# Attention scores in 64-row halves, product weights in 32-column tiles, and the values of two key tiles in one go

## The chip, the cores and the metric

The kernel runs on one core of a Trainium2 chip. Its engines work side by side and wait for each other through semaphores: TensorE (PE, matrix products; PEld is its weight load), VectorE (DVE), ScalarE (ACT), GpSimd (POOL) and SyncE (SP), which issues most DMAs. The metric is device time in microseconds (us), the median of several runs. Matrix products write to PSUM, which has eight banks of 128 partitions by 512 f32 numbers; DVE and ACT read them there.

## The reference

The input x is (2, 1024, 128). After a layer norm, the output is x plus an RWKV layer (a recurrence over time and a channel mix) plus an attention layer whose four projections are mixtures of experts. The costly part is the attention:

```
q = svd_moe(xn, q...) * SCALE; k = svd_moe(xn, k...); v = svd_moe(xn, v...)   # 16 heads of 8 numbers
attn = softmax(einsum('bhsd,bhtd->bhst', q, k), axis=-1)                      # 1024 x 1024 per head
ctx = einsum('bhst,bhtd->bhsd', attn, v)
out = svd_moe(ctx, o...)
x = x + rwkv_layer(xn) + out
```

With 2 batches there are 32 heads, so 32 score matrices of 1024 by 1024 in f32.

## The kernel before

The heads are worked on in 16 **pairs** (`PAIRS`), four sets of operands deep (`SETS`). Each f32 number of q and k is split into three bf16 parts, and the nine products of parts are stacked as rows: 72 rows of `q_op` and `k_op` for each of a pair's two heads `e`. Each pair goes through TensorE twice.

**A scores** (`fill_place`, L1091): queries on the output's partitions, 512 keys along the free axis, in bf16, 96 rows by 128 columns of weights. There are 32 of them in a pair (2 heads, 8 query tiles, 2 halves of the keys). DVE reduces each bank to a negated row maximum (`read_place`, L986). A 33rd "place" (k = 2 of the next pair) transposes the combined maxima of the pair on TensorE (L1084); DVE copies them out (L982, `max_rows`), POOL splits them in three bf16 parts (`split_max`, L564 to L570), and SP puts these as three more rows into `q_op` by DMA (`place_max`, L397). Places take turns on three banks (`A_BANK` and the two behind it), so a place waits until DVE has read the place three turns earlier.

**B scores** (`scores`, L1166): keys on the output's partitions, 512 queries along the free axis, 99 rows of weights, so that the scores come out less their maximum. A **step** is one tile of 128 keys; a pair has 8 steps. In a step there are two calls, one for each head, of two products each. Each call fills two banks, which ACT turns into exponentials with one instruction (`exps`, L804, 128x1024). A call waits until ACT has read the same two banks in the step before.

**Values** (`values`, L1176): v (32 columns of weights, f32) times the exponentials, four products with outputs on partitions 0, 32, 64 and 96 of one bank (`PV_BANK`), summed over the 8 steps. The row of ones in v gives the sum of the exponentials. Those of a step are issued in the following step. ACT copies the finished bank out (`copy_ctx`, L810) and SP stores it (`store_ctx`, L410).

In each step `one_step` of TensorE runs: place, B scores of head 0, place, B scores of head 1, place, values of the step before, remaining place. The places of a step belong to the next pairs: they run `LEAD` = 12 places plus one pair ahead, so 45 places stand in a prologue before the first step, interleaved with the RWKV projections (`project`, L1100 and L1112).

The RWKV recurrence is worked on beside it, in four **quarters** of four pairs (32 steps t = 0 to 31) by `branch(t, q)` of DVE, ACT and POOL. It has 8 TensorE products per quarter (`product`, `PRODUCT_STEP`: mean at t = 17, var 18, cr 22, ck0 23, ck1 25, ck2 26, ck3 27, cv 29, the last made of four), f32 with 128 x 128 weights, which take a turn on the three A banks. Each engine's program is written out by hand, in order; an instruction that waits holds up all that stands behind it on its engine. `program` runs three quarters in a loop and the last one unrolled, then `tail`.

SP's program per pair: store the context of the pair before, load the operands of pair p+3 (`load_pair`, 4 DMAs), stage v of p+1 (`stage_v`, 2 DMAs, L403), place the maxima of p+1 (3 DMAs).

Of the kernel before, what the change touches and what calls it, by code (L numbers as in the profile page):

```python
# [15 lines left out]
ROWS = PARTS * PARTS * HD  # L16
MAX_ROW = 96
# [3 lines left out]
LEAD = 12  # L21
SPLIT_STEP = 5
# [24 lines left out]
def build(nc, x, cols, mats, rows, gw1, gb1, gw2, gb2, out):  # L47
# [4 lines left out]
    with ctx:  # L52
# [55 lines left out]
        q_op = sb("q_op", [P, SETS, 2, T], BF16)  # L108
        k_op = sb("k_op", [P, SETS, 2, T], BF16)
        v_op = sb("v_op", [P, 2, KEY_TILES, 2, 32])  # L110
        probs = sb("probs", [P, 4, 2, CHUNK])

        res = probs[:, :, :, :].rearrange("p (t n) h c -> p t (n h) c", t=2)
        neg_half = sb("neg_half", [P, 2, KEY_TILES * 2 * 2])
        neg_max = sb("neg_max", [P, 2, KEY_TILES * 2])
        max_rows = sb("max_rows", [2 * KEY_TILES, 2, P])
# [3 lines left out]
        ctx_sb = sb("ctx_sb", [P, 2, CHUNK])  # L120
# [3 lines left out]
        ctx_dram = nc.dram_tensor("ctx_dram", [PAIRS, 4, HD + 1, CHUNK], F32).ap()  # L124
# [131 lines left out]
        op_in = [[sem(f"op_in{s}{e}") for e in range(2)] for s in range(SETS)]  # L256
# [19 lines left out]
        rec = sb("rec", [P, B, QT])  # L276
# [25 lines left out]

        def exists(it, pair, k):


            n = it * SETS + pair
            if not isinstance(n, int):
                return True
            return 1 <= n <= PAIRS if k == 2 else n < PAIRS

        def a_count(it, pair, k):

            n = it * SETS + pair
            if isinstance(n, int) and n == 0:
                return k if k < 2 else k - 1
# [8 lines left out]
        for t in range(SETS * KEY_TILES):  # L324
            at = A_PLACES + LEAD
            here = places(at + A_PLACES * t // KEY_TILES, at + A_PLACES * (t + 1) // KEY_TILES)
            place_turns.append(range(len(turns), len(turns) + len(here)))
            turns += here
            turns += [name for name, step in PRODUCT_STEP.items() if step == t]
        assert (len(turns) + 1) % 3 == 0  # L330
# [50 lines left out]
        def _(sp):  # L381
            def load_pair(p, s):


                for e in range(2):
                    sp.dma_start(q_op[0:ROWS, s, e, :],
                                 bass.AP(q_dram.tensor, (p * 2 + e) * (PARTS * HD * T),
                                         [[0, PARTS], [T, PARTS * HD], [1, T]])).then_inc(op_in[s][e], 16)
                    sp.dma_start(k_op[0:ROWS, s, e, :],
                                 bass.AP(k_dram.tensor, (p * 2 + e) * (SLOTS * HD * T),  # L390
                                         [[HD * T, PARTS], [T, PARTS * HD], [1, T]])).then_inc(op_in[s][e], 16)
# [879 lines left out]
```

## Time and profile before

| | |
|---|---|
| median of 3 runs | 528.16 us (526.9 to 528.55) |
| span of the profiled execution | 526.2 us |
| PE, DVE, ACT, POOL busy | 470.9, 407.4, 356.4, 183.4 us |
| span up to the first A score | 69.2 us |
| prologue of A scores, to the first B score | 69.2 to 97.8 us |
| the 16 pairs | 97.8 to 507.5 us |
| output projection and stores | 507.5 to 526.2 us |

The profile describes one execution; the medians are of others and lie 2.0 us above its span. A busy TensorE in these tables is not TensorE at its peak, since its products overlap and their ends are modelled: the distance from the start of one product to the start of the next is the better measure. The chain that ended last is followed back from the last instruction, at each step to what released it.

### The profile page before, as it was taken

What the parts mean: (1) busy time and instruction counts of PE and PEld (TensorE: products, weight loads), DVE (VectorE), ACT (ScalarE), POOL (GpSimd) and SP (SyncE); (2) the same over time, 40 slices, a digit from 0 to 9 for tenths busy, and PEclk for the clock granted to TensorE, in tenths of its full rate; (3) what the DMA queues carried; (4) which work ended last, traced back from release to release, by engine and by line L of the source; (5) the groups of instructions that cost most, each with busy time, mean ns of one, the idle gap of its engine ahead of it and who ended that gap; (6) DMA issues with size and microseconds to landing.
All of it is one profiled execution on the core that took longest, in us unless ns stands there. A gap on an engine that the chain in (4) does not pass through costs nothing.

```text
span 526.2 us, 8110 instructions
## 1 busy us (share of the span) xinstructions
PE 470.9 (89%) x2358; PEld 160.8 (31%) x2358; DVE 407.4 (77%) x668; ACT 356.4 (68%) x452; POOL 183.4 (35%) x214
## 2 busy tenths in 40 slices
PE   5339379999999999999999999999999999999992
PEld 3115123232233332222333322223333223232252
DVE  3578989999888868998887689998876899981022
ACT  3865212578968756789788567887775678878851
POOL 9556900331534221315432303153323031634200
PEclk9859769999999999999999999999999999999996
DMA  6001326110111110101101001111010111010205
GB/s 211 0 1 56 121 75 208 30 25 12 48 32 27 33 25 10 46 24 33 36 20 38 19 15 41 27 30 43 14 45 11 22 37 12 1 13 1 87 7 159
DMA packets 49289, 22.25 MB, mean 42 GB/s; under 512 B 36532, under 2 KB 40756, under 8 KB 49268
## 3 DMA queue, kind: packets, MB, share of 16 engines
q1 hardware_dynamic: 48736, 21.83, 15.3%
q10 hardware_dynamic: 532, 0.16, 0.3%
q8 instruction: 11, 0.18, 0.2%
q14 instruction: 10, 0.08, 0.0%
HBM read 14.31 MB, written 6.42 MB: 39 GB/s over the span
## 4 chain that ended last, share of the span: by engine, by line
PE 69%; DVE 16%; ACT 5%; issue 5%; DMA 3%; POOL 1%; SPq 1%; DVEq 0%; POOLq 0%; ACTq 0%
PE banks L1091 19%; PE banks L1176 19%; PE banks L1166 17%; DVE neg_half L986 6%; PE banks L1159 3%; ACT probs L804 3%; PE banks L1155 3%; DVE run L945 2%; DVE probs L917 1%; PE banks L1112 1%; PE banks L1100 1%; DMA x_sb<-in_x_dram 1%; DVE parts L921 1%; DVE parts L919 1%; DVE parts L915 1%
## 5 line engine op out<-in xcount | busy, mean ns | idle before, releaser
L986 DVE TENSOR_REDUCE neg_half<-banks 128x1 f32<-128x512 f32 x512 | 323.7, 685 | 46.1 <-PE banks L1091 44.3
L804 ACT ACTIVATE probs<-banks 128x1024 f32<-128x1024 f32 x256 | 247.5, 1021 | 74.4 <-PE banks L1166 73.6
L1091 PE MATMUL banks<-k_op,q_op 96*128 96x512 bf16 x512 | 181.2, 384 | 19.7 <-DVE V L937 11.4
L1166 PE MATMUL banks<-q_op,k_op 99*128 99x512 bf16 x512 | 151.5, 379 | 1.2 <-DMA q_op<-max_parts 0.6
L1176 PE MATMUL banks<-probs,v_op 128*32 128x512 f32 x1024 | 136.4, 605 | 0.4 <-ACT probs L804 0.4
L1091 PEld LDWEIGHTS banks<-k_op,q_op 96*128 96x128 bf16 x512 | 43.6, 97 | 170.0 <-DVE neg_half L986 126.3
L1166 PEld LDWEIGHTS banks<-q_op,k_op 99*128 99x128 bf16 x512 | 49.0, 98 | 65.3 <-issue 11.9
L1176 PEld LDWEIGHTS banks<-probs,v_op 128*32 128x32 f32 x1024 | 20.1, 108 | 53.5 <-issue 52.3
L643 POOL TENSOR_TENSOR qk_f<-qk_f 128x512 f32<-128x512 f32 x12 | 12.5, 1039 | 52.6 <-ACT qk_f L789 52.6
L968 DVE TENSOR_TENSOR rec<-banks,parts 128x512 f32<-128x512 f32 x4 | 2.8, 692 | 34.6 <-PE banks L1155 34.6
L564 POOL TENSOR_TENSOR max_parts<-max_rows,zero_rows 16x128 bf16<-16x128 f32 x16 | 7.1, 444 | 56.7 <-DVE max_rows L982 56.3
L597 POOL TENSOR_TENSOR xc<-run 128x512 f32<-128x512 f32 x4 | 4.2, 1039 | 48.4 <-DVE run L945 48.4
L742 ACT ACTIVATE sq<-banks 128x512 f32<-128x512 f32 x4 | 2.4, 598 | 22.0 <-PE banks L1100 22.0
L1159 PE MATMUL banks<-xc,mat_sb 128*128 128x512 f32 x32 | 16.8, 606 | 0.0
L602 POOL TENSOR_TENSOR qk_f<-qk_f 128x512 f32<-128x512 f32 x4 | 5.1, 1276 | 33.4 <-ACT qk_f L757 33.4
L789 ACT ACTIVATE qk_f<-banks 128x512 f32<-128x512 f32 x12 | 7.2, 597 | 11.2 <-PE banks L1159 11.2
L1112 PE MATMUL banks<-hT,u_s 128*128 128x512 f32 x24 | 13.2, 631 | 0.0
L1100 PE MATMUL banks<-hT,u_s 128*128 128x512 f32 x24 | 12.6, 607 | 0.0
L610 POOL TENSOR_TENSOR hT<-qk_f,hT 128x512 f32<-128x512 f32 x4 | 5.1, 1278 | 19.4 <-ACT hT L763 19.4
L606 POOL TENSOR_TENSOR hT<-qk_f,parts 128x512 f32<-128x512 f32 x4 | 5.1, 1280 | 18.9 <-ACT qk_f L763 18.9
L1015 DVE TENSOR_TENSOR parts<-parts 128x512 f32<-128x512 f32 x4 | 2.8, 693 | 11.4 <-ACT parts L830 11.4
L579 POOL TENSOR_TENSOR xc<-xc,run 128x512 f32<-128x512 f32 x8 | 9.3, 1183 | 5.6 <-ACT xc L784 5.6
(163 smaller groups left out, 456.0 us busy)
## 6 DMA issues: line engine op xcount, KB each, us to landing
q_op<-q_dram SPq DMA_DIRECT2D x32, 144.0 KB
k_op<-k_dram SPq DMA_DIRECT2D x32, 144.0 KB
k_dram<-parts SPq DMA_DIRECT2D x10, 256.0 KB, 3.9
parts<-ctx_dram SPq DMA_DIRECT2D x8, 256.0 KB, 4.2
mat_sb<-in_mats_dram SPq DMA_DIRECT2D x2, 768.0 KB, 7.7
q_dram<-parts SPq DMA_DIRECT2D x6, 256.0 KB, 3.2
ctx_dram<-ctx_sb SPq DMA_DIRECT2D x64, 18.0 KB
x_sb<-in_x_dram SPq DMA_DIRECT2D x4, 256.0 KB, 5.6
```

What stands on the lines that cost most here:

```text
L579: g.tensor_tensor(mix_in[i][:, :, :], mix_in[i][:, :, :], prev, ALU.add).then_inc(mixed, 1)
L643: g.tensor_tensor(kk[i][:, :, :], kk[i][:, :, :], kk[i][:, :, :], ALU.mult).then_inc(kk_ready, 1)
L804: a.activation(probs[:, (2 * step + e) % 4, :, :], banks[:, 2 * e:2 * e + 2, :], ACT.Exp).then_inc(b_read, 1)
L945: v.tensor_tensor_scan(out_[:, b, 1:], c0[:, b, :], data1, out_[:, b, 0:1], op0, op1).then_inc(done, 1)
L986: v.tensor_reduce(neg_half[:, s, u:u + 1], src, axis=AX.X, op=ALU.max, negate=True).then_inc(a_read, 1)
L1091: mm(dst, q_op[0:MAX_ROW, s, e, P * c:P * c + P], k_op[0:MAX_ROW, s, e, CHUNK * h:CHUNK * h + CHUNK], start=True, stop=True).then_inc(a_re ...
L1100: mm(project_bank(m), w_mix[:, i, 1, :], hT[:, n // 2, at:at + CHUNK], start=False, stop=True).then_inc(kvr_ps, 1)
L1112: mm(project_bank(m), w_mix[:, i, 0, :], hT[:, n // 2, at:at + CHUNK], start=True, stop=False)
L1155: last = mm(dst, mat(f"cv{i}"), flat(kk[i]), start=(i == 0), stop=(i == 3))
L1159: mm(dst, mat(name), flat(mix_in[1]), start=True, stop=True).then_inc(ck_ps, 1)
L1166: last = mm(bank(2 * e + h), k_op[0:MAX_ROW + PARTS, s, e, P * step:P * step + P], q_op[0:MAX_ROW + PARTS, s, e, CHUNK * h:CHUNK * h + CHU ...
L1176: last = mm(banks[g:g + 32, PV_BANK, :], v_op[:, s % 2, step, e, :], probs[:, (2 * step + e) % 4, h, :], start=(step == 0), stop=(step == ...
```

## The change

- **Operands.** `q_op` and `k_op` become `q_main` and `k_main`, in which head 0 stands on partitions 0 to 63 and head 1 on 64 to 127 (64 of the 72 rows), and `q_tail` and `k_tail` (two sets deep), in which each half holds the last 8 rows and, from row 32 of the half, the three rows of maxima.
- **A scores** use the 64 main rows alone. Places alternate between the heads (`place_of`), and come in units of two, one unit before the B scores of a step and one behind them. The transpose is place 4 instead of 2 and stands behind the second unit of step 4.
- **B scores.** A call now covers both heads for one half of the queries: main rows of head 0, of head 1, then tail rows of head 0, of head 1, added into the same banks: 8 products per step instead of 4.
- **Values** are issued in even steps alone, for the two steps before, so `probs` has 8 slots instead of 4.
- **Products** (mean to cv) are cut into four products with 32 columns of weights each.
- **LEAD** is 17 instead of 12 (50 places in the prologue), `SPLIT_STEP` 4 instead of 5.
- **DMAs per pair**: `load_pair` 8 in two halves around the others (was 4), `load_tail` 4 (new), `place_max` 6 (3), `stage_v` 1 (2), `store_ctx` 1 of 256 KB (4 of 18 KB). `ctx_sb`, `rec` and `max_rows` move into buffers that are free by then. The first memsets are smaller.

The core of the diff (buffers, constants and the DMA code that the list above tells are left out):

```diff
-LEAD = 12
-SPLIT_STEP = 5
+LEAD = 17
+UNITS = 16
+LEAD_UNITS = 8
+TURN_PLACE = 4
+SPLIT_STEP = 4
...
-        probs = sb("probs", [P, 4, 2, CHUNK])
+        probs = sb("probs", [P, 8, 2, CHUNK])
...
+        def unit_places(unit):
+            at = 2 * unit + (2 * unit >= TURN_PLACE)
+            return at, at + 1
+        def place_of(k):
+            u = k if k < TURN_PLACE else k - 1
+            return u % 2, u // 4, u // 2 % 2
...
             def place_max(p, s):
                 sp.wait_ge(max_parts_ready, p + 1)
                 for i in range(PARTS):
-                    sp.dma_start(q_op[MAX_ROW + i:MAX_ROW + i + 1, s, :, :],
-                                 max_parts[:, s % 2, i, :]).then_inc(max_in[s % 2], 16)
+                    for e in range(2):
+                        sp.dma_start(q_tail[HALF * e + MAX_ROW + i:HALF * e + MAX_ROW + i + 1, s % 2, :],
+                                     max_parts[KEY_TILES * e:KEY_TILES * (e + 1), s % 2, i, :]
+                                     ).then_inc(max_in[s % 2], 16)
...
-                mm(dst, q_op[0:MAX_ROW, s, e, P * c:P * c + P],
-                   k_op[0:MAX_ROW, s, e, CHUNK * h:CHUNK * h + CHUNK],
+                e, c, h = place_of(k)
+                if k < 2:
+                    pe.wait_ge(main_in[s][e], (it + pair // SETS + 1) * 64)
+                mm(dst, q_main[HALF * e:HALF * (e + 1), s, P * c:P * c + P],
+                   k_main[HALF * e:HALF * (e + 1), s, CHUNK * h:CHUNK * h + CHUNK],
                    start=True, stop=True).then_inc(a_ready, 1)
...
+                def columns(weights, moving, start=True, stop=True):
+                    for g in range(0, P, 32):
+                        last = mm(dst[g:g + 32, :], weights[:, g:g + 32], moving, start=start, stop=stop)
+                    return last
...
-            def scores(p, s, step, e):
+            def scores(p, s, step, h):
                 if not (first(p) and step == 0):
-                    pe.wait_ge(b_read, p * 16 + 2 * step + e - 1)
-                for h in range(2):
-                    last = mm(bank(2 * e + h), k_op[0:MAX_ROW + PARTS, s, e, P * step:P * step + P],
-                              q_op[0:MAX_ROW + PARTS, s, e, CHUNK * h:CHUNK * h + CHUNK], start=True, stop=True)
+                    pe.wait_ge(b_read, p * 16 + 2 * step + h - 1)
+                for q_rows, k_rows, used, of in ((q_main, k_main, HALF, s), (q_tail, k_tail, MAX_ROW + PARTS, s % 2)):
+                    for e in range(2):
+                        last = mm(bank(2 * h + e), k_rows[HALF * e:HALF * e + used, of, P * step:P * step + P],
+                                  q_rows[HALF * e:HALF * e + used, of, CHUNK * h:CHUNK * h + CHUNK],
+                                  start=(q_rows is q_main), stop=(q_rows is q_tail))
                 last.then_inc(b_ready, 1)
...
             def one_step(p, j, it, step):
-                fill_turn(it, todo[0])
+                for turn in todo[0]:
+                    fill_turn(it, turn)
...
                 scores(p, j, step, 0)
-                fill_turn(it, todo[1])
                 scores(p, j, step, 1)
-                fill_turn(it, todo[2])
...
-                if step > 0:
+                for turn in todo[1]:
+                    fill_turn(it, turn)
...
+                if step > 0 and step % 2 == 0:
+                    values(p, j, step - 2)
                     values(p, j, step - 1)
-                elif not first(p):
+                elif step == 0 and not first(p):
+                    values(p - 1, (j - 1) % SETS, KEY_TILES - 2)
                     values(p - 1, (j - 1) % SETS, KEY_TILES - 1)
-                for turn in todo[3:]:
-                    fill_turn(it, turn)
```

TensorE's order in the first pair of the loop, before. L1091 is an A score, L1166 the B scores of one head, L1176 the values of one step; the register instructions work out the numbers for waits:

```order
L1176 MATMUL banks<-probs,v_op 32x512 x4
L353 REGISTER_ALU
L1091 MATMUL banks<-k_op,q_op 128x512
L353 REGISTER_ALU
L1091 MATMUL banks<-k_op,q_op 128x512
L1164 REGISTER_ALU
L1166 MATMUL banks<-q_op,k_op 128x512 x2
L353 REGISTER_ALU
L1091 MATMUL banks<-k_op,q_op 128x512
L1164 REGISTER_ALU
L1166 MATMUL banks<-q_op,k_op 128x512 x2
```

TensorE's order at the end of an even step of the same pair in the changed kernel (L1134 is an A score, L1216 the B scores, L1227 the values of two steps):

```order
L1216 MATMUL banks<-q_main,k_main 128x512 x2
L1216 MATMUL banks<-q_tail,k_tail 128x512 x2
L377 REGISTER_ALU
L1134 MATMUL banks<-k_main,q_main 128x512
L377 REGISTER_ALU
L1134 MATMUL banks<-k_main,q_main 128x512
L1245 ISA
L1227 MATMUL banks<-probs,v_op 32x512 x8
L377 REGISTER_ALU
L1134 MATMUL banks<-k_main,q_main 128x512
L377 REGISTER_ALU
L1134 MATMUL banks<-k_main,q_main 128x512
```

Before, four value products stand between two A scores in each step; now eight do in every second step, and the A scores of a step stand in two pairs around its B scores.

SyncE's order in the same pair before, from staging v (L403) over the rows of maxima (L397) to storing the context (L410):

```order
L403 DMA v_op<-V 128x8x8
L403 ISA
L403 DMA v_op<-V 128x8x8
L395 REGISTER_ALU
L397 DMA q_op<-max_parts 1x16x128 x3
L410 ISA
L410 DMA ctx_dram<-ctx_sb 9x512
```

The same stretch in the changed kernel, from staging v (L442) over the tails (L426, L428) and the maxima (L436) to the second half of the loads (L412):

```order
L442 DMA v_op<-V 128x16x8
L426 ISA
L426 DMA q_tail<-q_dram 8x1024
L428 ISA
L428 DMA k_tail<-k_dram 8x1024
L426 ISA
L426 DMA q_tail<-q_dram 8x1024
L428 ISA
L428 DMA k_tail<-k_dram 8x1024
L433 REGISTER_ALU
L436 DMA q_tail<-max_parts 1x8x128 x6
L412 ISA
```

Four short loads now stand ahead of the maxima, the maxima are six DMAs, and half of the operand loads stand behind them.

## Rows read from the trace of the kernel before

**Rows 1.** The page: engines' busy time; chain by engine.

```profile
PE 470.9 (89%) x2358; PEld 160.8 (31%) x2358; DVE 407.4 (77%) x668; ACT 356.4 (68%) x452; POOL 183.4 (35%) x214
...
PE 69%; DVE 16%; ACT 5%; issue 5%; DMA 3%; POOL 1%; SPq 1%; DVEq 0%; POOLq 0%; ACTq 0%
```

**Rows 2.** Busy time by stretch: prologue's start, then a quarter, mean to mean.

```profile
50.00:75.00 25.00, 13.56 (x37) 6.10 (x37) 22.36 (x33) 3.62 (x6) 14.97 (x11) 0.73 0.37 121
...
151.36:255.64 104.28, 102.00 (x539) 31.78 (x538) 88.19 (x145) 78.09 (x93) 33.76 (x42) 1.00 0.12 29
```

**Rows 3.** Timeline of TensorE and DVE (start, length, what, [idle before]), one step and a product.

```profile
251.58 1.06 PE L1176 MATMUL banks<-probs,v_op 128*32 128x512 f32 x8
...
252.58 0.61 PE L1091 MATMUL banks<-k_op,q_op 96*128 96x512 bf16 x2
...
253.02 0.60 PE L1166 MATMUL banks<-q_op,k_op 99*128 99x512 bf16 x2
...
253.46 0.38 PE L1091 MATMUL banks<-k_op,q_op 96*128 96x512 bf16 x1
...
253.67 0.59 PE L1166 MATMUL banks<-q_op,k_op 99*128 99x512 bf16 x2
...
254.11 0.38 PE L1091 MATMUL banks<-k_op,q_op 96*128 96x512 bf16 x1
...
254.42 1.07 PE L1176 MATMUL banks<-probs,v_op 128*32 128x512 f32 x8
...
255.41 0.39 PE L1091 MATMUL banks<-k_op,q_op 96*128 96x512 bf16 x1
...
255.64 1.02 PE L1145 MATMUL banks<-qk_f,mean_w 128*128 128x512 f32 x2
...
255.84 0.69 DVE L986 TENSOR_REDUCE neg_half<-banks 128x1 f32<-128x512 f32 x1 [0.35 <-PE banks L1091]
...
256.50 0.38 PE L1091 MATMUL banks<-k_op,q_op 96*128 96x512 bf16 x1
```

**Rows 4.** Timeline of DVE's reads, the two scans of t = 2 and a bank refilled.

```profile
74.60 16.24 DVE L986 TENSOR_REDUCE neg_half<-banks 128x1 f32<-128x512 f32 x27 [0.53 <-PE banks L1091]
...
106.08 1.38 DVE L945 TENSOR_TENSOR_SCAN run<-parts,run,col_sb 128x256 f32<-128x256 f32 x2
...
107.38 5.06 DVE L986 TENSOR_REDUCE neg_half<-banks 128x1 f32<-128x512 f32 x8
...
108.10 0.39 PE L1091 MATMUL banks<-k_op,q_op 96*128 96x512 bf16 x1 [0.16 <-DVE neg_half L986]
```

**Rows 5.** Timeline of ScalarE: the exponentials of one step.

```profile
257.35 1.94 ACT L804 ACTIVATE probs<-banks 128x1024 f32<-128x1024 f32 x2 [1.76 <-PE banks L1166]
```

**Rows 6.** Groups of ScalarE and DVE in the quarter 151.36 to 255.64.

```profile
L763 ACT ACTIVATE qk_f<-qk_f 128x512 f32<-128x512 f32 x3 | 1.9, 629 | 0.1
...
L968 DVE TENSOR_TENSOR rec<-banks,parts 128x512 f32<-128x512 f32 x1 | 0.7, 691 | 3.2 <-PE banks L1155 3.2
```

**Rows 7.** Timeline: the first maxima, from the transpose to the first B score.

```profile
91.21 0.27 PE L1084 MATMUL banks<-ident,neg_max 128*16 128x128 f32 x1
...
94.12 0.42 POOL L570 TENSOR_TENSOR max_parts<-max_res,max_parts 16x128 bf16<-16x128 f32 x1
...
94.56 1.88 SPq L397 DMA_DIRECT2D q_op<-max_parts  x3
...
97.83 0.59 PE L1166 MATMUL banks<-q_op,k_op 99*128 99x512 bf16 x2
```

**Rows 8.** Timeline of ScalarE: context copies behind the last pair of a quarter and two pairs later.

```profile
204.59 0.59 ACT L810 COPY ctx_sb<-banks 128x512 f32<-128x512 f32 x1
...
252.71 0.59 ACT L810 COPY ctx_sb<-banks 128x512 f32<-128x512 f32 x1
```

**Rows 9.** Timeline: start and end of the last pair's steps 1 to 7.

```profile
485.12 1.33 PE L1166 MATMUL banks<-q_op,k_op 99*128 99x512 bf16 x4
...
506.52 1.06 PE L1176 MATMUL banks<-probs,v_op 128*32 128x512 f32 x8 [0.36 <-ACT probs L804]
```

More of the change, by code:

```diff
@@ L255, in build @@
         parts_out = [sem(f"parts_out{b}") for b in range(B)]
-        op_in = [[sem(f"op_in{s}{e}") for e in range(2)] for s in range(SETS)]
+        main_in = [[sem(f"main_in{s}{e}") for e in range(2)] for s in range(SETS)]
+        tail_in = [sem(f"tail_in{s}") for s in range(2)]
         v_in = [sem(f"v_in{s}") for s in range(2)]
@@ L324, in build @@
         for t in range(SETS * KEY_TILES):
[L325 to L328, printed above, removed]
+            here = []
+            for half in range(2):
+                ahead, unit = divmod(LEAD_UNITS + 2 * (t % KEY_TILES) + half, UNITS)
+                pair = t // KEY_TILES + 1 + ahead
+                here.append([(pair, k) for k in unit_places(unit)])
+                if unit == TURN_PLACE // 2 - 1:
+                    here[-1].append((pair, TURN_PLACE))
+            place_turns.append((range(len(turns), len(turns) + len(here[0])),
+                                range(len(turns) + len(here[0]), len(turns) + len(here[0]) + len(here[1]))))
+            turns += here[0] + here[1]
             turns += [name for name, step in PRODUCT_STEP.items() if step == t]
+        assert turns[0] == divmod(A_PLACES + LEAD, A_PLACES)
         assert (len(turns) + 1) % 3 == 0
@@ L801, in exps @@
             def exps(p, step):
-                for e in range(2):
-                    act.wait_ge(b_ready, p * 16 + 2 * step + e + 1)
-                    a.activation(probs[:, (2 * step + e) % 4, :, :], banks[:, 2 * e:2 * e + 2, :],
+                for h in range(2):
+                    act.wait_ge(b_ready, p * 16 + 2 * step + h + 1)
+                    a.activation(probs[:, (2 * step + h) % 8, :, :], banks[:, 2 * h:2 * h + 2, :],
                                  ACT.Exp).then_inc(b_read, 1)
@@ L1154, in product @@
                         pe.wait_ge(kk_ready, q * 4 + i + 1)
-                        last = mm(dst, mat(f"cv{i}"), flat(kk[i]), start=(i == 0), stop=(i == 3))
+                        last = columns(mat(f"cv{i}"), flat(kk[i]), start=(i == 0), stop=(i == 3))
                     last.then_inc(cv_ps, 1)
@@ L1176, in values @@
                         last = mm(banks[g:g + 32, PV_BANK, :], v_op[:, s % 2, step, e, :],
-                                  probs[:, (2 * step + e) % 4, h, :], start=(step == 0), stop=(step == KEY_TILES - 1))
+                                  probs[:, (2 * step + h) % 8, e, :], start=(step == 0), stop=(step == KEY_TILES - 1))
                 last.then_inc(pv_done, 1)
@@ L1211, in tail @@
             def tail():
+                values(PAIRS - 1, SETS - 1, KEY_TILES - 2)
                 values(PAIRS - 1, SETS - 1, KEY_TILES - 1)
```

122 lines of the change are left out of this document (69 added, 53 removed).

## Prediction

> **What bounds the kernel now.** I read the engines' busy time and the chain by engine first [rows 1]: TensorE holds 69% of the chain, and DVE, which looks almost as loaded in the pairs, only 16%. Then the busy time by stretch [rows 2]: a quarter (four pairs, from one mean product to the next) takes 104.28 us, TensorE is busy for 102.0 of it at a granted clock of 1.00 (the 2.4 GHz level), DVE for 88.2, ACT for 78.1. Then the timeline of a step [rows 3]. From value product to value product, 251.58 to 254.42, is 2.84 us. In it four A scores take 0.22 us each (253.46 to 253.67, the next product's start), the two calls of B scores 0.43 each, and the values 0.99 (254.42 to 255.41). Adding up: 4 x 0.22 + 2 x 0.43 + 0.99 = 2.73, and 0.1 more between the last A score and the values (254.11 + 0.22 to 254.42). The values' own stream is two passes of 0.43, as in the f32 product of the mean, which takes 0.86 (255.64 to 256.50); so a visit to the values costs 0.86 and about 0.24 of changing over (0.10 in, 0.14 out).
> DVE in the same step reads four banks. Its reads stand 0.60 apart: 27 of them in 16.24 us, the last 0.69 long [rows 4]. That is 2.4 of 2.84 us. So TensorE sets the pace of the pairs, DVE is 15% behind it, and the two are tied by only three banks.
>
> **Halves.** TensorE loses work. If two products on different row halves run at the same time, two A scores cost 0.22 instead of 0.43, and the eight B products of a step cost 4 x 0.22, as the four did. No row shows row halves; the nearest are the values, whose eight products (four by four on different columns) have a mean of 0.6 each and yet leave after 0.99 [rows 3]. They also show that TensorE can issue a product every 0.11 us, which is what 4 B products in 0.43 need. I take full overlap. In two steps TensorE then needs 8 A scores 0.87, B scores 1.74, values 1.71 and one change over 0.24: 4.56 instead of 5.68 us. Were that all, a quarter would shrink by 16 x 1.1 = 18 us.
>
> **Where that gain goes.** DVE's own need in two steps is 8 x 0.60 = 4.8 us, and it can't read while TensorE is in the values, beyond the three banks that are full. I walk through two steps, from T, the start of DVE's read of the first place behind the values. The reads start at T, T+0.6, ... The eighth place, the last before the values, needs the bank of the fifth, whose read starts at T+2.40 and is over 0.69 later; TensorE reuses a bank 0.03 after that (107.38 + 0.69 = 108.07, next A score at 108.10 [rows 4]). So it starts at T+3.12, and the values 0.31 later (254.11 to 254.42 [rows 3]) at T+3.43. They last 1.71 and 0.14 to leave: the next A score starts at T+5.28, and DVE reads it 0.43 after its start (255.41 to 255.84 [rows 3]), at T+5.71. DVE ends its eighth read at T+4.9 and idles 0.8. Two steps take **5.71 us, against 5.68 now**. The faster products change nothing in this loop: only the refill of a bank, the doubled values and the first fill are in it. The B scores fit in: those of the odd step start at T-0.2 and are followed by 1.94 us of exponentials [rows 5], which end near T+2.4, and the second call of the even step starts then, before T+3.12. ACT's 3.9 us of exponentials fit in 5.7, and with eight slots they go on during the values.
>
> **A quarter, summed.** Sixteen double steps: 91.4. The transpose now follows the eighth place, so the values wait for one more read, 0.6, and the combining of the maxima before it costs DVE about 0.3: 4 x 0.9 = 3.6. The three pairs of scans (1.38 us each [rows 4]) are in even steps and so behind the eighth read, in DVE's idle 0.8: 0.5 each stays, 1.5. The subtraction after the mean product: 0.6. Products in odd steps (mean, ck0, ck1, ck3) stand where DVE has three full banks to read: fourth place at T+0.7, product 0.1 later, over at T+2.0, fifth place readable at T+2.5, when DVE is just through: nothing. Products in even steps (var, cr, ck2) stand behind the values and add their 0.86: 2.6. cv, four products, 3.4 us behind the fourth place, then two DVE operations of 0.69 [rows 6]: the fifth read starts at T+6.0 instead of T+2.4, 3.5. In steps 9 to 12 ACT has two more activations of 0.63 [rows 6] per step, 8 x 0.63 + 4 x 1.94 = 12.8 against 11.4 for two double steps: 1.5. Sum: 91.4 + 3.6 + 1.5 + 0.6 + 2.6 + 3.5 + 1.5 = **104.7**, against 104.3. Over three quarters that is +1.2.
>
> **Start and end.** The first B score (97.83) waits for the first maxima, 6.6 us after their transpose at 91.21 [rows 7]. The transpose comes two places later (+1.2); three more row DMAs, at 0.63 each from 1.88 for three, add 1.9; the projections between the A scores change the array's division about twice per five places, which I put at 0.1 for each of 8 stretches, +0.8. Sum +3.9. The five places more that DVE reads before (3.0) lie within that. The last quarter: its first two pairs have the scans, ACT's load and two transposes but none of the odd-step products that pay for them: 8 x 5.71 + 2 x 0.9 + 3 x 0.5 + 1.5 = 50.5 against 48.1 now (from context copy to context copy, 204.59 to 252.71 [rows 8]), +2.3. Its last two have fewer A scores, which were done earlier: steps without places cost about 5.0 per two (exponentials to scores to exponentials: 2 x 1.0 + 0.6 before the second call, the values' 1.95 behind it), plus 0.86 for each even product; I get 21.8 us for the last pair from its step 1 against 22.4 (485.12 to 507.5 [rows 9]) and 1.2 less in the one before: -1.8.
> Smaller terms at nothing: the shorter memsets (POOL idles before its first use of the data), product weights in 32 columns (eight small weight loads hide as the values' do; if they don't, 0.1 x 11 per quarter), the context store of 256 KB in one DMA (fewer issues, longer transfer; between -1 and +1 once). Sum: 526.2 + 1.2 + 3.9 + 2.3 - 1.8 = **531.8 us** of span; with the 2.0 that the median lies above the span now, **533.8**.
>
> **Loads.** SP has to place the maxima in time. After the transpose (step 4): 0.7 for the read, 2.0 for POOL as before (91.21 + 1 to 94.5), 3.8 for six DMAs, 1.2 to land (96.44 to 97.6 [rows 7]); the scores that need them come 10.4 us after the transpose by the walk above. 1.9 us are left, if the staging of v and the four tails ahead of them are through.
>
> **A rule against it.** The rows above say that DVE's reads and the three banks decide. By this rule, the trace agrees: the Trainium skill, TensorEngine Tiling (Array Packing), section PSUM Bottleneck, says that tiling speeds up TensorE but not the evacuation of PSUM, which can become the bound. Taken alone it would bound two steps at DVE's 4.8 us, an estimate of about 90 us per quarter; the walk gives 5.71 and 104.7, because the fills are held off too. Its section Key Properties says that a change of the tiling mode drains TensorE. The rows show one such change, at 0.24 for in and out; none shows one between row halves and column tiles.
>
> **The rivals.** *Faster, 517.* DVE's side work hides altogether (scans in the idle 0.8, ACT's excess in its slack, transpose among the banks) and the change over costs 0.1 less: -1.5 -1.5 -1.6 per quarter, -4.6, over 3.8 quarters -17. For it: TensorE has over 1 us of slack per two steps. Against: nothing shortens the bank cycle itself. Chance 0.22.
> *Slower, 550.* The change between row halves and column tiles costs twice what the one in the trace does: +0.24 per two steps, 3.8 per quarter, 15 in all, and 1.5 in the prologue. It decides from the first double visit, since it lies in the 5.71 one to one. Chance 0.17.
> *The halves don't overlap, about 624.* The change does not do what it says: two steps cost TensorE 8 x 0.22 + 16 x 0.22 + 1.95 = 7.2 instead of 5.7, +24 per quarter, +90. Against it: columns do overlap. Chance 0.06.
> *The maxima come late, 549.* Tails or slower issue push the six DMAs past their 1.9 us: at 1 us more each pair, +15. Chance 0.08.
>
> *The clock.* From 50 to 75 us, where TensorE is busy for 13.6 of 25 us with one long wait, its granted clock is 0.73 on average [rows 2]. With 1.1 us less to do in 5.7 it still works 80% of the time, in gaps of about 1 us at most; I keep the 2.4 GHz level and count a fall within the 0.17 of the slower case.
>
> **Numbers.** My forecast, 533.8, has 0.47, with 527 to 542 of its own (change over from -0.05 to +0.1 per visit, the prologue between +2 and +6). A kernel like this is told from no change at about 0.3%, 1.6 us. Faster (below 526.6): the first rival and 0.04 of the forecast, 0.26. Same: 0.12. Slower: 0.62. The range from 514 to 552 leaves out the case without overlap and somewhat under half of the fastest, 0.16 in all.
>
> **What would show it.** In the profile after: TensorE busy well below its 89%, the mean clock still 1.00 in the pairs; DVE idle before its reads some 0.8 to 0.9 in every second step and none in the other, so that DVE, not TensorE, holds the chain; value groups of 16 records 1.7 to 1.9 long every 5.7 us; quarters of 104 to 105 us; the first B score near 101.7. It is wrong if two steps without products are not 5.7 us: 5.0 or less would mean that the reads don't wait for the values, 6 that changing over is dearer. If A scores of a unit start 0.22 apart with free banks, the halves don't overlap. TensorE waiting for the tails' or maxima's DMA at the head of pairs would be the loads.

## The result, and the profile after

The changed kernel takes **553.42 us** (median of 4 runs, 552.72 to 554.29) against 527.53 us of the kernel before on the same chip: a ratio of 1.0482, with an interval of 1.0455 to 1.0510. That is slower, as forecast, but by 26 us and not by 6, and just outside the range of 514 to 552. The profiled execution has a span of 552.3 us; before it was 526.2 and forecast were 531.8.

The page of the changed kernel answers [rows 1]: TensorE's busy time, the clock granted to it in 40 slices, the queue that brings in instructions (packets, MB, share), the chain by engine, and DVE's reads (busy, mean | idle before them, releaser).

```profile
PE 465.1 (84%) x3134; PEld 158.2 (29%) x3134; DVE 396.3 (72%) x668; ACT 356.3 (65%) x452; POOL 178.1 (32%) x213
...
PEclk9859869779999999799999996999999989999998
...
q8 instruction: 32, 0.52, 0.4%
...
PE 57%; DVE 25%; issue 7%; DMA 4%; ACT 4%; SPq 1%; DVEq 0%; ACTq 0%
...
L1030 DVE TENSOR_REDUCE neg_half<-banks 128x1 f32<-128x512 f32 x512 | 316.3, 683 | 79.1 <-PE banks L1134 78.5
```

As the walk said, DVE now idles behind TensorE's A scores (78.5 of its 79.1 us), and holds 25% of the chain instead of 16%. But TensorE still holds 57%: the sign that I had named, DVE and not TensorE holding the chain, did not come. Not foreseen are the dips of the clock in four places from the first pair on (slices 8 and 9, 17, 25 and 33), the 7% of "issue", and the 32 loads of instructions, where the kernel before has 11.

**The steady steps came out as walked.** Timeline of the changed kernel (start, length, what, [idle before]); it answers [rows 3]:

```profile
251.01 1.92 PE L1227 MATMUL banks<-probs,v_op 128*32 128x512 f32 x16
...
252.86 0.39 PE L1134 MATMUL banks<-k_main,q_main 64*128 64x512 bf16 x2
...
253.09 0.38 PE L1216 MATMUL banks<-q_main,k_main 64*128 64x512 bf16 x2
...
253.29 2.48 DVE L1030 TENSOR_REDUCE neg_half<-banks 128x1 f32<-128x512 f32 x4 [0.89 <-PE banks L1134]
```

The doubled values last 1.85 from their start to the next A score (the walk had 1.71 and 0.14). Two A scores on different row halves take 0.23 together (252.86 to 253.09). DVE idles 0.89 before the first read behind the values (the walk had 0.8).

**The time went at two places.** The table takes the context copies (ScalarE, one at the end of each pair, [rows 8]) as marks:

| stretch | before | forecast | after |
|---|---|---|---|
| span to the first B score | 97.8 | 101.7 | 105.6 |
| first B score to first context copy | 26.1 | 26.1 | 31.2 |
| first to last copy (15 pairs) | 383.7 | 385.4 | 398.9 |
| last copy to the end | 18.6 | 18.6 | 16.7 |

Within the third line most pairs are within 0.8 us of those before; three are not. The pair behind the first jump takes 30.25 us (217.00 to 247.25), where before it took 24.37 (204.59 to 228.96); behind the second jump it is 31.2, and where the loop is left, without a jump back, 25.85. Timeline of TensorE and ScalarE there:

```profile
214.91 1.92 PE L1227 MATMUL banks<-probs,v_op 128*32 128x512 f32 x16
...
217.00 0.58 ACT L853 COPY mat_sb<-banks 128x512 f32<-128x512 f32 x1 [0.70 <-PE banks L1227]
...
218.97 0.50 PE L1134 MATMUL banks<-k_main,q_main 64*128 64x512 bf16 x2 [2.14 <-issue]
...
222.30 1.00 PE L1134 MATMUL banks<-k_main,q_main 64*128 64x512 bf16 x3 [1.96 <-issue]
...
247.25 0.58 ACT L853 COPY mat_sb<-banks 128x512 f32<-128x512 f32 x1 [0.73 <-PE banks L1227]
```

The chain of waits from 216 to 232 us, by line and its first pieces (start, length, what):

```profile
by line: issue 29.9%; PE banks L1216 21.5%; PE banks L1227 20.5%; PE banks L1134 17.3%; DVE neg_half L1030 12.9%; DVE neg_max L1034 0.4%; DVEq L1029 0.2%
...
216.83 2.14 issue
218.97 0.50 PE banks L1134 x2
219.47 0.87 PE banks L1216 x8
220.34 1.96 issue
222.30 0.59 PE banks L1134
```

Twice TensorE stands still for 2 us, waiting for nothing that the profile shows (behind the second jump for 2.18 and 0.81 us), and between 216 and 224 us the instruction queue moves two packets:

```profile
q8 instruction: 2, 0.03, 2.2%
```

That is not all of it: right behind the halts the granted clock falls. Stretches of the changed kernel (busy time and count of PE, PEld, DVE, ACT and POOL, granted clock, DMA share, GB/s):

```profile
99.00:105.00 6.00, 3.65 (x12) 0.82 (x10) 5.91 (x11) 1.23 (x2) 3.27 (x7) 0.97 0.01 2
105.40:119.00 13.60, 12.88 (x60) 4.31 (x61) 9.26 (x16) 5.81 (x6) 2.08 (x3) 0.53 0.14 25
151.00:176.00 25.00, 23.17 (x177) 7.51 (x177) 20.36 (x36) 20.14 (x25) 14.47 (x16) 1.00 0.16 39
221.50:228.00 6.50, 5.34 (x26) 1.76 (x29) 4.39 (x8) 2.32 (x3) 0.00 (x0) 0.54 0.11 38
330.00:340.30 10.30, 9.13 (x41) 2.70 (x39) 6.36 (x10) 3.88 (x4) 1.18 (x2) 0.51 0.10 29
449.50:453.00 3.50, 3.50 (x19) 0.62 (x20) 1.10 (x3) 0.56 (x1) 1.72 (x4) 0.53 0.00 0
```

From 221.5 to 228 and, behind the second jump, from 330 to 340.3 the clock is at the 1.2 GHz level. The same happens from 105.4 to 119, over the first pair: 13.6 us at 0.53. Ahead of it, from 99 to 105, TensorE is busy for 3.65 of 6 us only. From 151 to 176 it is 1.00. The last row is the pair where the loop is left: no halt stands there, only 3.5 us at 0.53, and this is its extra 1.5 us. A run below has the same fall with no load of instructions near it, so it can't be laid to the loads. What makes it is open; with the loop kept, other runs have it elsewhere or not at all.

### The profile page after: what moved, and what is told of

Read it like the earlier page. It is cut to its first block, busy times and chain, and to the rows that moved or that the text cites. A ratio compares the mean times of both kernels' runs of the same rounds, so it can differ in the third digit from the quotient of the medians.

```text
span 552.3 us, 9871 instructions
## 1 busy us (share of the span) xinstructions
PE 465.1 (84%) x3134; PEld 158.2 (29%) x3134; DVE 396.3 (72%) x668; ACT 356.3 (65%) x452; POOL 178.1 (32%) x213
## 3 DMA queue, kind: packets, MB, share of 16 engines
q1 hardware_dynamic: 51104, 24.85, 16.7%
## 4 chain that ended last, share of the span: by engine, by line
PE 57%; DVE 25%; issue 7%; DMA 4%; ACT 4%; SPq 1%; DVEq 0%; ACTq 0%
PE banks L1227 19%; DVE neg_half L1030 17%; PE banks L1216 12%; PE banks L1134 12%; PE banks L1189 7%; ACT probs L847 2%; DVE run L988 2%; PE banks L1143 2%; PE banks L1155 2%; DMA x_sb<-in_x_dram 1%; DMA k_main<-k_dram 1%; DMA parts<-ctx_dram 1%; PE banks L1083 1%; DVE parts L964 1%; DMA k_dram<-parts 1%
## 5 line engine op out<-in xcount | busy, mean ns | idle before, releaser
L1030 DVE TENSOR_REDUCE neg_half<-banks 128x1 f32<-128x512 f32 x512 | 316.3, 683 | 79.1 <-PE banks L1134 78.5
L1134 PE MATMUL banks<-k_main,q_main 64*128 64x512 bf16 x512 | 139.7, 398 | 44.1 <-DVE neg_half L1030 23.8
L1227 PE MATMUL banks<-probs,v_op 128*32 128x512 f32 x1024 | 128.9, 622 | 0.6 <-ACT probs L847 0.6
L1216 PE MATMUL banks<-q_main,k_main 64*128 64x512 bf16 x512 | 111.0, 390 | 4.6 <-ACT probs L847 4.3
L1216 PE MATMUL banks<-q_tail,k_tail 35*128 35x512 bf16 x512 | 110.8, 389 | 0.0
L1134 PEld LDWEIGHTS banks<-k_main,q_main 64*128 64x128 bf16 x512 | 41.4, 95 | 190.7 <-DVE neg_half L1030 120.1
L1227 PEld LDWEIGHTS banks<-probs,v_op 128*32 128x32 f32 x1024 | 27.4, 112 | 59.3 <-issue 45.6
L1216 PEld LDWEIGHTS banks<-q_tail,k_tail 35*128 35x128 bf16 x512 | 33.3, 97 | 21.3 <-issue 2.2
L1216 PEld LDWEIGHTS banks<-q_main,k_main 64*128 64x128 bf16 x512 | 28.0, 96 | 38.2 <-ACT probs L847 22.5
L607 POOL TENSOR_TENSOR max_parts<-u_s,zero_rows 16x128 bf16<-16x128 f32 x16 | 11.0, 687 | 60.4 <-DVE u_s L1025 60.4
L1189 PE MATMUL banks<-xc,mat_sb 128*32 128x512 f32 x160 | 21.1, 600 | 1.9 <-DVE neg_half L1030 1.9
L853 ACT COPY mat_sb<-banks 128x512 f32<-128x512 f32 x16 | 9.4, 585 | 11.1 <-PE banks L1227 11.1
L1189 PE MATMUL banks<-qk_f,mat_sb 128*32 128x512 f32 x96 | 11.1, 596 | 0.6 <-DVE neg_half L1030 0.6
```

The costliest lines, as they stand in the source:

```text
L607: g.tensor_tensor(m0, rows_, zero_rows[:, :], ALU.add).then_inc(max_part, 1)
L853: a.copy(ctx_sb[:, s % 2, :], bank(PV_BANK)).then_inc(ctx_copied, 1)
L1030: v.tensor_reduce(neg_half[:, s, u:u + 1], src, axis=AX.X, op=ALU.max, negate=True).then_inc(a_read, 1)
L1134: mm(dst, q_main[HALF * e:HALF * (e + 1), s, P * c:P * c + P], k_main[HALF * e:HALF * (e + 1), s, CHUNK * h:CHUNK * h + CHUNK], start=True ...
L1189: last = mm(dst[g:g + 32, :], weights[:, g:g + 32], moving, start=start, stop=stop)
L1216: last = mm(bank(2 * h + e), k_rows[HALF * e:HALF * e + used, of, P * step:P * step + P], q_rows[HALF * e:HALF * e + used, of, CHUNK * h:C ...
```

## The experiments

The theory from these rows: the walk is right, and the loss has two causes outside it, instruction loads at the jump (some 12 to 14 us) and the clock in the first pair (some 4). The rivals: the jump's pairs are long for their place in the pattern of products, not for the jump; and doubled values are dearer than walked.

**The loop undone.** All 16 pairs written out, nothing else changed:

```diff
-            with eng.Fori(0, PAIRS // SETS - 1) as it:
-                for j in range(SETS):
-                    rest(it * SETS + j, j, it)
-                    head(it * SETS + j + 1, (j + 1) % SETS, it + (j + 1) // SETS)
-            for p in range(PAIRS - SETS, PAIRS):
+            for p in range(PAIRS):
```

> The changed kernel with all 16 pairs written out, no loop on any engine. Theory 'jump': in the changed kernel the first pair of each later loop pass takes 30.3 and 31.2 us instead of the 24.9 of my sum, since TensorE's loop body no longer stays loaded (16 KB instruction loads go on through all passes, 32 instead of 11), TensorE stands still twice for 2 us behind the jump, and then runs at half clock for 7 to 10 us. Without a jump both go: 553 less 5.4 and 6.3, 541 to 542. Rival 'pair start': the loss belongs to that pair's work (windows, maxima, context store), and the time stays at 553.

539.5 us, ratio 1.0249 (1.0200 to 1.0298), 14 less than with the loop. Its page and its context copies:

```profile
q8 instruction: 25, 0.41, 0.3%
...
PE 50%; DVE 38%; DMA 4%; ACT 4%; SPq 1%; issue 1%; DVEq 0%; ACTq 0%
```

```profile
215.37 0.59 ACT L849 COPY mat_sb<-banks 128x512 f32<-128x512 f32 x1 [0.60 <-PE banks L1223]
...
239.68 0.59 ACT L849 COPY mat_sb<-banks 128x512 f32<-128x512 f32 x1 [0.71 <-PE banks L1223]
```

The pair in question now takes 24.31 us, a quarter 104.27 (forecast 104.7), and "issue" is 1% of the chain. The place in the pattern is out: the jump costs the time. 25 loads in a row, without a jump, cost nothing that can be seen: from first to last context copy it is 383.5 us, against 383.7 before.

**Values in every step.** `values` once per step, as before; halves, tiles, slots and loop stay:

```diff
-                if step > 0 and step % 2 == 0:
-                    values(p, j, step - 2)
+                if step > 0:
                     values(p, j, step - 1)
-                elif step == 0 and not first(p):
-                    values(p - 1, (j - 1) % SETS, KEY_TILES - 2)
+                elif not first(p):
                     values(p - 1, (j - 1) % SETS, KEY_TILES - 1)
```

> The changed kernel, but the values of one step in every step, as before, instead of two steps' in every second. Theory 'banks': the doubled visit is what takes back the gain of the halves, since DVE runs dry behind three banks. With single visits TensorE needs 2 x 0.22 + 0.87 + 0.86 + 0.24 = 2.4 us per step and DVE 4 x 0.60 = 2.4, so two steps take 4.9 instead of 5.7 us; a quarter shrinks by some 11 us with the products as they are, the whole by about 40: 510 to 516, with the stalls at the jumps unchanged. Rival 'changing over': twice as many changes between row halves and column tiles cost as much as the banks give, 548 to 556. Rival 'exponentials': ACT sets 2.8 us per step, 545 to 553.

526.8 us, ratio 1.0004 (0.9973 to 1.0036): 27 us less than with doubled values, short of the 40 expected. Timeline of the values:

```profile
256.34 1.07 PE L1227 MATMUL banks<-probs,v_op 128*32 128x512 f32 x8
...
258.83 1.06 PE L1227 MATMUL banks<-probs,v_op 128*32 128x512 f32 x8
...
261.32 1.06 PE L1227 MATMUL banks<-probs,v_op 128*32 128x512 f32 x8
```

A plain step falls to 2.49 us from 2.84: with the values short, the halves pay. In the pair with ScalarE's extra activations three steps take 3.0 to 3.6 (the pair 22.3, where eight plain steps would be 19.9), and ACT holds 10% of the chain. Part of the rest of the 40 stays there, the other part in the two pairs with most products (24.6 and 28.2). The loads are still 32, and the pair behind the jump takes 29.1.

**The prologue's spacing.** `PROJECT_GAP` says after how many places the next two projections come. With 6 instead of 5 they reach to the end of the 50 places:

```diff
-PROJECT_EARLY, PROJECT_FROM, PROJECT_GAP = 4, 2, 5
+PROJECT_EARLY, PROJECT_FROM, PROJECT_GAP = 4, 2, 6
```

> The changed kernel with the projections of the prologue spread over 50 places instead of 42 (one of each kind per 6 places instead of 5). Theory 'idle before the loop': with 17 places of lead the last 8 or so places have no projection between them, TensorE streams only 0.22 of every 0.60 us from 99.5 to 105 us, and the clock falls to half from 105.4 to 119. With the projections spread the clock holds and the time falls by 4 to 7 us, to 546 to 549. Rival 'load wait': the fall comes from the halt before the first B scores (the maxima's six DMAs) or from the entry into the loop, and the time stays at 552 to 554.

549.15 us, ratio 1.0431 (1.0365 to 1.0496), span 548.0. The same two stretches in it:

```profile
99.00:105.00 6.00, 5.60 (x16) 1.69 (x17) 5.37 (x10) 0.60 (x1) 1.72 (x4) 1.00 0.01 3
105.00:119.00 14.00, 11.62 (x79) 4.36 (x77) 13.69 (x24) 9.15 (x11) 5.21 (x8) 1.00 0.16 30
```

With TensorE busy for 5.60 of the 6 us ahead, the clock stays at 1.00, and 79 products instead of some 60 run in the 14 us behind. The first B score comes 1.9 later, the first pair is 4.5 shorter, and the span 4.3. Only 2.6 of these 4.3 are there by the first context copy (134.09 against 136.71). Another 1.6 are the pair where the loop is left, which takes 24.21 here and has no fall of the clock; whether the spacing has to do with that is not shown.

**A longer loop body, first try.** To see whether the length of the loop is what counts, 13 empty instructions were put into each step of the kernel before:

```diff
                 fill_turn(it, todo[0])
+                for _ in range(13):
+                    pe.nop()
```

> The kernel before with 13 empty instructions added to every step of TensorE, some 416 per loop body, so that its body is as long as the changed one's; nothing else. Theory 'jump': its two later passes then begin with the same stalls and the same fall of the clock, +10 to +12 in all, 537 to 541, and the instruction loads go on through all passes. Rival: length doesn't matter, 528; or the empty instructions cost time themselves, evenly in all pairs, up to 0.03 x 13 x 128 = 50 us.

528.44 us, ratio 1.0008 (0.9979 to 1.0036). The empty instructions were not in the program that was built (as many instructions and 11 loads as before), so this is the kernel before once more and tells nothing of the length.

**All three changes.** No loop, single values, gap 6, each edited as above:

> The changed kernel with three edits together: no loop, the values of one step in every step, projections spread over the 50 places. If the three losses are separate (jumps 11 to 14 us by the first run, doubled values 27, half clock before the loop 4), it is 553 - 13 - 27 - 4 = 509, between 506 and 513, below the kernel before by over 2%. If they share a cause (the clock, above all), it stays at 515 or more.

**510.89 us** (5 rounds), ratio 0.9677 (0.9641 to 0.9713). It beats both kernels; the gains add up. One quarter, and DVE's reads on its page:

```profile
205.86:303.49 97.63, 93.37 (x736) 26.91 (x734) 86.54 (x145) 77.64 (x95) 34.79 (x42) 1.00 0.16 39
```

```profile
L1026 DVE TENSOR_REDUCE neg_half<-banks 128x1 f32<-128x512 f32 x512 | 319.3, 683 | 29.6 <-PE banks L1130 28.1
```

**The loop undone in the kernel before**, by the same edit as in the changed one, since part of that gain could be the loop's alone:

> The kernel before with all pairs written out: the control to the runs without a loop. Its loop passes show no stall (three quarters of 104.28 us alike), so both theories expect 526 to 529; were it faster by several us, the gain without a loop would not be peculiar to the changed kernel.

525.98 us, ratio 0.9967 (0.9943 to 0.9992). The old loop costs under 2 us. So the change with single values and the wider gap is worth 15 us over a kernel before that is also written out.

**A shorter body.** Single values with the loop, but products 128 columns wide again, which takes TensorE's instructions per pass from 1694 to 1562:

```diff
-                    for g in range(0, P, 32):
-                        last = mm(dst[g:g + 32, :], weights[:, g:g + 32], moving, start=start, stop=stop)
-                    return last
+                    return mm(dst, weights[:, 0:P], moving, start=start, stop=stop)
```

> The changed kernel with the loop, values in every step, and the products mean to cv with 128 columns of weights, as before, instead of four times 32: TensorE's loop body has 1547 instructions by the program's order instead of 1679 (before: 1292). It measures what the product tiles cost (my sum: nothing, an f32 product streams for 0.86 us either way) and whether a body of 1547 stays loaded. If it doesn't: 525 to 529 as with tiles. If it does, the stalls go, 12 less: 513 to 517, with some 11 to 13 instruction loads instead of 32.

521.28 us, ratio 0.9864 (0.9828 to 0.9899). 13 loads in all, and the pair behind the jump takes 22.9 instead of 29.1. But only 5.5 us are left of a gain of 12: wide products cost some 6 (from first to last context copy 366.4 us, against 360.4 with all three changes). Values, product and the next A score in it, and in the run with all three changes:

```profile
262.93 1.07 PE L1225 MATMUL banks<-probs,v_op 128*32 128x512 f32 x8
263.93 1.13 PE L1188 MATMUL banks<-xc,mean_w 128*128 128x512 f32 x2
264.99 0.39 PE L1134 MATMUL banks<-k_main,q_main 64*128 64x512 bf16 x2
```

```profile
256.07 1.06 PE L1223 MATMUL banks<-probs,v_op 128*32 128x512 f32 x8
256.95 1.04 PE L1185 MATMUL banks<-xc,mean_w 128*32 128x512 f32 x8
257.93 0.39 PE L1130 MATMUL banks<-k_main,q_main 64*128 64x512 bf16 x2
```

2.06 us against 1.86 from the values to the A score: I read this as the array changing nothing between two groups of column tiles, which the rows don't show by themselves. A quarter takes 99.2 us with wide products and 97.6 with tiles.

**A longer body in the kernel before.** A product of 2 columns, whose result is overwritten, ahead of each A score and each call of B scores, which makes 1686 instructions per pass:

```diff
+                mm(dst[:, 0:2], q_op[0:MAX_ROW, s, e, P * c:P * c + P],
+                   k_op[0:MAX_ROW, s, e, CHUNK * h:CHUNK * h + 2], start=True, stop=True)
                 mm(dst, q_op[0:MAX_ROW, s, e, P * c:P * c + P],
```

> The kernel before with a product of two columns ahead of every A score and of every call of B scores, into a bank that is overwritten at once: TensorE's loop body has 1676 instructions instead of 1292. Theory 'jump': the instruction loads rise from 11 to 30 or so, and the first pair of the second and third pass is 4 to 6 us longer than the first pair of the last quarter, with two halts of TensorE of about 2 us. Rival: length doesn't matter, the first pairs of all quarters are alike. The small products themselves cost up to 0.03 x 6 per step, evenly, 0 to 25 us in all.

556.95 us (one run). Not by halts: there are 14 loads, none of them between 200 and 435 us, and the pairs behind the two jumps take 25.25 us each, that behind the loop's end, where no jump is taken back, 25.16. The first of them:

```profile
212.37 0.59 ACT L810 COPY ctx_sb<-banks 128x512 f32<-128x512 f32 x1
...
237.62 0.59 ACT L810 COPY ctx_sb<-banks 128x512 f32<-128x512 f32 x1
```

That is 0.9 us more than before (24.37); the other pairs of the quarter are 1.0 to 3.7 longer than theirs. The small products cost far more than expected, but not at the jump. Part of their price is the clock: in the second pair of each pass it falls (0.54 from 365 to 370 us). For the length this is a refutation: 1686 instructions stay loaded, 1694 do not. Eight more are an unlikely limit. What else differs is where the body begins: at TensorE's 480th instruction here, at the 402nd in the changed kernel. Loads come in 16 KB (32 of them are 0.52 MB), and the changed kernel without loop needs 25 of them for 3134 products and as many weight loads, some 250 instructions each; with TensorE's other instructions, 6393 in all, it is 256, or 64 bytes for one. A body of 1694 lies in seven such blocks or in eight, by where it begins.

**The same body, moved.** The changed kernel with 44 products of 2 columns (88 instructions) in the prologue. The body keeps its 1694 instructions and begins at the 490th:

```diff
+                if small:
+                    mm(dst[:, 0:2], q_main[HALF * e:HALF * (e + 1), s, P * c:P * c + P],
+                       k_main[HALF * e:HALF * (e + 1), s, CHUNK * h:CHUNK * h + 2], start=True, stop=True)
```

> The changed kernel, loop body untouched (1694 TensorE instructions per pass by the trace), with a product of two columns ahead of 44 of the 50 prologue places, which moves the body by 88 instructions. The runs so far: bodies of 1302, 1562 and 1686 stay loaded, 1694 does not. Theory 'blocks': instructions come in loads of 16 KB, 256 instructions; what counts is how many blocks the body touches. Starting 402 instructions in, 1694 touch eight; the longer kernel of before starts at 480 and its 1686 may touch seven. From these two the body touches seven once it starts 78 to 98 later. Then the loads fall from 32 to 14 or so, both stalls at the jumps go, and the time falls by 12 less what the small products cost (1 to 3): 541 to 545. Rival 'limit': a body over some 1690 instructions never stays, 32 loads, 553 to 557.

542.07 us, ratio 1.0276 (1.0234 to 1.0317), 11.4 less than the changed kernel, although work was added. Loads, the jump and the pair behind it:

```profile
q8 instruction: 14, 0.23, 0.2%
```

```profile
216.25 1.92 PE L1230 MATMUL banks<-probs,v_op 128*32 128x512 f32 x16
218.10 0.39 PE L1137 MATMUL banks<-k_main,q_main 64*128 64x512 bf16 x2
```

```profile
218.34 0.59 ACT L853 COPY mat_sb<-banks 128x512 f32<-128x512 f32 x1 [0.70 <-PE banks L1230]
...
244.26 0.59 ACT L853 COPY mat_sb<-banks 128x512 f32<-128x512 f32 x1 [0.72 <-PE banks L1230]
```

No halt stands behind the jump (values at 216.25, A score at 218.10), and the pair takes 25.9 instead of 30.25. The 1.6 that it is still above 24.3 are a short fall of the clock (0.58 from 229 to 232.5), with no load between 205 and 425 us; behind the second jump the pair takes 24.31, and where the loop is left 24.21. Length as such is out; the place of the body in the program decides. That it is seven blocks against eight fits all five bodies if some 32 to 86 instructions, which the trace does not list, lie ahead of the first; the border itself was not looked for, so the rule stays an explanation that foretold one run.

**The price of doubled values by itself.** The changed kernel without loop and with gap 6, which differs from the fastest version in the values alone:

> The changed kernel without a loop and with spread projections, values still doubled: the partner of the run with all three edits (510.9), for the doubled values' price without stalls and without the clock's fall. If it is the bank cycle alone: two steps 5.7 against 4.9 us where ACT leaves room, less in steps with much ACT work, 24 to 27 in all, 535 to 538. If the doubled values' price came partly from the stalls, less: 525 to 532.

536.18 us, ratio 1.0168 (1.0126 to 1.0209). Against 510.89 that makes **25.3 us** for issuing the values of two key tiles together (24.4 of it between the first B score and the last context copy). Its reads and its chain:

```profile
L1026 DVE TENSOR_REDUCE neg_half<-banks 128x1 f32<-128x512 f32 x512 | 315.5, 680 | 60.4 <-PE banks L1130 59.4
...
PE 48%; DVE 40%; DMA 4%; ACT 4%; SPq 2%; issue 1%; DVEq 0%; ACTq 0%
```

DVE idles 59.4 us behind A scores instead of 28.1, more than the 25.3; both runs have the same clock in their quarters (1.00), the same halves and the same loads (25). This fits the bank cycle of the walk: three banks full, TensorE away for 1.85, DVE out of work for 0.89. The number of banks itself was not varied.

## Why the prediction was right and wrong

**Two steps in 5.71 us: right.** Each part is in the timeline: the visit of 1.85, the idle 0.89, and without the jump a quarter of 104.27 us where the sum gave 104.7; from first to last context copy the loop-free version takes 383.5 us and the kernel before 383.7. So the small loss that I forecast there did not come, but its reason, that doubled values eat what the halves save, stands.

**The quarter's sum: right in total, partly by luck.** Its first two pairs take 48.0 us in the loop-free version (24.31 and 23.72), where my terms, as I added them for the last quarter, make 50.5. ScalarE's excess (1.5) costs nothing, and the scans (1.5) about 0.6, the difference between the two pairs. The other two take 56.2 (26.54 and 29.70), where the terms leave 54.2: the products cost 2 us more than I gave them. The two errors cancel. In the last quarter they don't: its first two pairs take what they did before (+2.3 forecast), and its last two take 0.6 more than before (-1.8 forecast).

Neither the rival with the dearer change over (the visit has the old 0.14) nor the halves that don't overlap came, nor the faster rival with its 100 us a quarter. The slower rival's 550 us lies near the measured time, but its cause is absent: that is chance.

**The jump: no term at all.** This is the step that failed. The sum prices what stands in the order of instructions, and I took each instruction as there when its turn comes. The diff adds four B products per step and cuts the wide products in four: 1302 instructions per pass become 1694. It costs 11.4 us (moved body) to 13.9 (no loop). By the pairs, the two jumps cost 5.9 and 6.9 us; of these 4.1 and 3.0 are halts, and the rest comes with the clock that falls behind them. The page of before shows the instruction queue with its 11 loads, and I never asked what 392 more instructions per pass would do to it. The Trainium skill, Runtime: NRT & Kernel Launch, section Instruction fetch mechanics, says that TensorE has 128 KiB for instructions (2048 of them), refilled in blocks of 16 KiB, and that a taken branch whose target is not in the current two-page window has to wait for a fetch. By the first, the new body should fit; here it did only when moved. By the second, the trace agrees as to the halts, 2.14 and 1.96 us, but not as to the window: bodies of 1302, 1562 and 1686 instructions, far longer than two such blocks, were jumped back over without a halt.

**"I keep the 2.4 GHz level": wrong behind the prologue.** I looked at the steady steps, where it holds (1.00), and not at the end of the prologue, where `LEAD` of 17 puts A scores past the last projection. There they come 0.60 apart, TensorE is busy for 3.65 of 6 us, and the first pair runs 13.6 us at 1.2 GHz. It lasts 31.2 us instead of 26.1. With the gap closed it is 4.5 shorter, of which 2.6 us are left at the first context copy.

**The start: +3.9 forecast, +7.7 measured to the first B score.** The transpose comes at 96.46 instead of 91.21, 5.25 later, where I had 2.0. I had missed that places which alternate between the heads need both heads' operands at once:

```profile
71.98 0.61 PE L1134 MATMUL banks<-k_main,q_main 64*128 64x512 bf16 x2 [2.59 <-DMA k_main<-k_dram]
72.52 2.07 PE L1155 MATMUL banks<-hT,u_s 128*128 128x512 f32 x2
```

The second A score waits 2.59 us for head 1's half of the load, and the projections begin at 72.52 instead of 70.41. That is 2.1 of the 5.25. The first round of places and projections takes 0.8 more, the next five 0.9 (3.2 us each instead of 3.0), and the last stretch before the transpose 1.5, since a projection more comes before it. From transpose to first B score it is 9.10 against 6.62: +2.5 where I had 1.9. The six DMAs themselves were close:

```profile
99.95 4.12 SPq L436 DMA_DIRECT2D q_tail<-max_parts  x6
```

4.12 us instead of 3.8 forecast. In the fastest version the first context copy still comes 7 us later than before (131.0 against 124.0). This part was not tried on its own, beyond the wider gap.

**The end: -1.8, not looked for.** From the last context copy to the end it takes 16.7 us instead of 18.6. The kernel before is at a granted clock of 0.61 from 515 to 526 us, the changed one at 0.89 from 536 to 552; whether that is the reason stays open.

**Maxima in time: right.** No pair behind the first waits for its rows of maxima. The margin of 1.9 us in the prediction is added up wrongly: 0.7 + 2.0 + 3.8 + 1.2 is 7.7, and 2.7 are left of 10.4.

Added up from the forecast span of 531.8: the two pairs behind the jumps and the one where the loop is left +14.4 (30.25, 31.2 and 25.85 us against 24.3 each), first pair +5.0, start +3.9, end -1.8, all other pairs -0.9: 552.4, with 552.3 measured.

## What to carry to other kernels

Where a change adds instructions to a loop, count them per pass and per engine, and look in the profile at the queue that loads instructions: here its packets grew from 11 to 32, the engine stopped at each jump, and TensorE paid a second time by its clock. The limit of a body's length was not measured; the place of the body in the program mattered as well. Where two engines hand over few PSUM banks, short visits elsewhere are worth more than fewer visits: doubling a visit of 0.99 saved one change over of 0.24 and cost 25 us in all. Ask of each stretch in which TensorE works in gaps, the end of a prologue above all, what clock the stretch behind it will get.

## What the runs showed of the hardware

- A loop body of 1694 TensorE instructions was loaded anew in each pass (32 loads of 16 KB in all, halts of 2.14 and 1.96 us at the first jump, 2.18 and 0.81 at the second) when it began at the engine's 402nd instruction, and stayed loaded (14 loads) when it began at the 490th.
- Behind the halts at the two jumps, and behind 6 us with 3.65 busy, TensorE's clock was at 1.2 GHz (granted 0.54, 0.51 and 0.53) for 6.5, 10.3 and 13.6 us, though the engine was busy most of that time (5.34 of 6.5, 9.13 of 10.3, 12.88 of 13.6).
- Two bf16 products of 512 columns on row halves 0 to 63 and 64 to 127 took 0.23 us together, and going back from column tiles to them cost the same 0.14 us as to full rows before.
- A 128-column f32 product between column tiles and the next A score cost 0.2 us more than the same product as four tiles of 32 columns (2.06 against 1.86 from the values' start).
- Products of 2 columns are not nearly free: 192 of them with their weight loads per pass of four pairs made the kernel before about 29 us longer (one run), part of it with the clock at 1.2 GHz.
